# The first blocks of a fused layer: one tile of rows ahead of the rest, loads in another order

## The reference

```python
x = x + tanh(g_xattn[0]) * L0_xattn(layernorm(x), ctx, ctx)   # softmax over q^T k / 16, per tile
x = x + tanh(g_ffn[0]) * L0_ffn(layernorm(x), W_syn, b_syn, W_out, b_out, gamma, beta)
x = x + tanh(g_xattn[1]) * L1_xattn(ctx, ctx, layernorm(x), ssm_kernel, D, 8)
x = x + tanh(g_ffn[1]) * L1_ffn(layernorm(x), gate_w, w_gate_up, w_down, ws_gate_up, ws_down)

# in L0_ffn
scale = mean(abs(W));  q = clip(round(W / (scale + 1e-8)), -1, 1) * scale   # ternary weights
z = x @ q.T + b_syn                                                         # 256 -> 1024, then the top 102 of a row are kept
out = layernorm(x + out, gamma, beta)
```

## Time and profile before

| | us |
|---|---|
| median of three runs | 744.54 |
| the profiled execution | 744.91 |
| its span | 742.8 |
| TensorE busy | 615.8 (83%) |
| VectorE busy | 478.2 (64%) |
| GpSimd busy | 433.9 (58%) |
| ScalarE busy | 285.2 (38%) |

### The profile page before, as it was taken

The page is one execution under the profiler, slowest core; times in us unless marked ns, Lnnn a source line. Parts: engine busy times, 40 slices in busy tenths (PEclk is TensorE's granted clock), DMA queues, the critical chain, the costliest instruction groups (busy, mean ns, idle before and its releaser), DMA issues.

```text
span 742.8 us, 12155 instructions
## 1 busy us (share of the span) xinstructions
PE 615.8 (83%) x3072; PEld 474.9 (64%) x3072; DVE 478.2 (64%) x1604; ACT 285.2 (38%) x641; POOL 433.9 (58%) x482
## 2 busy tenths in 40 slices
PE   3699994863998966999999649999999999999920
PEld 2355552532887744777777538888888888888620
DVE  3898997998687768688886433444455454455415
ACT  2146777873353432254444303233223223232200
POOL 2487997230244330677777651676767777777660
PEclk9999997897999987999999678999999999999965
DMA  6358655697387936476673379999999999997958
GB/s 216 106 188 263 225 190 199 213 318 278 116 328 258 386 100 235 156 243 214 218 235 137 106 245 302 264 247 238 251 257 248 242 265 252 263 248 161 233 85 310
DMA packets 89035, 167.84 MB, mean 226 GB/s; under 512 B 11280, under 2 KB 53712, under 8 KB 88976
## 3 DMA queue, kind: packets, MB, share of 16 engines
q1 hardware_dynamic: 67504, 138.44, 56.1%
q0 software_dynamic: 20608, 27.82, 18.9%
q10 hardware_dynamic: 864, 0.93, 0.3%
HBM read 93.33 MB, written 73.81 MB: 225 GB/s over the span
## 4 chain that ended last, share of the span: by engine, by line
PE 60%; DVE 17%; issue 9%; DMA 7%; POOL 3%; ACT 2%; DVEq 1%; SPq 0%; POOLq 0%; ACTq 0%
PE psum L1103 11%; PE psum L1021 6%; PE psum L1116 6%; PE psum L1107 5%; PE psum L942 5%; PE psum L1121 4%; PE psum L1087 3%; PE psum L863 3%; DVE hh L1679 3%; PE psum L1032 3%; DMA acc<-hh,toki 2%; POOL acc L806 2%; PE psum L978 2%; PE psum L933 2%; PE psum L835 1%
## 5 line engine op out<-in xcount | busy, mean ns | idle before, releaser
L806 POOL DMA_INDIRECT acc<-hh,toki x128 | 187.9, 1468 | 84.3 <-DVE hh L1994 47.9
L1994 DVE TENSOR_SCALAR hh<-psum,wtok 96x256 f32<-96x256 f32 (+3 forms) x128 | 55.9, 477 | 133.0 <-issue 118.2
L766 POOL DMA_INDIRECT xs_rows<-Z,slot x96 | 96.4, 1004 | 43.6 <-issue 26.0
L1103 PE MATMUL psum<-qT,Z 128*128 128x192 f32 (+3 forms) x480 | 99.8, 351 | 0.0
L1103 PEld LDWEIGHTS psum<-qT,Z 128*128 128x128 f32 x480 | 82.3, 193 | 2.9
L684 POOL TENSOR_TENSOR rstd<-mv,neghalf 128x1 f32<-128x1 f32 (+1 forms) x48 | 35.5, 739 | 80.0 <-DVE mv L1439 64.6
L1372 ACT ACTIVATE qT<-psum 128x384 f32<-128x384 f32 (+3 forms) x64 | 33.5, 523 | 97.0 <-PE psum L1087 96.1
L863 PE MATMUL psum<-wt,hTs 128*128 128x512 f32 x128 | 59.5, 607 | 0.6 <-ACT hTs L1201 0.6
L942 PE MATMUL psum<-wt,hh 128*128 128x256 f32 x256 | 57.9, 379 | 0.0
L1116 PE MATMUL psum<-Z,hh 128*96 128x256 f32 (+3 forms) x240 | 56.7, 379 | 0.0
L1107 PE MATMUL psum<-qT,Z 128*112 128x192 f32 (+3 forms) x240 | 53.5, 345 | 0.0
(11 more groups left out here) (350 smaller groups left out, 1257.8 us busy)
## 6 DMA issues: line engine op xcount, KB each, us to landing
Z<-in_wexp SPq DMA_DIRECT2D x62, 496.0 KB, 4.4
xs_rows<-fill SPq DMA_DIRECT2D x64, 272.0 KB, 3.2
kv_rows<-Z SPq DMA_DIRECT2D x12, 688.0 KB, 3.7
kvb<-kv_rows SPq DMA_DIRECT2D x8, 688.0 KB, 6.3
Z<-co_rows SPq DMA_DIRECT2D x8, 688.0 KB
Z<-kv_rows SPq DMA_DIRECT2D x8, 688.0 KB, 6.5
Z<-xs_rows SPq DMA_DIRECT2D x24, 204.0 KB, 3.9
Z<-xs_rows SPq DMA_DIRECT2D x16, 272.0 KB, 3.9
```

The source lines that it names most:

```text
L766: pool.indirect_dma_start(out=xs_rows[:, :], out_offset=bass.IndirectOffsetOnAxis(ap=slot[:, t, k:k + 1], axis=0), in_=H[:, t, :], in_offs ...
L806: pool.indirect_dma_start(out=acc[a][:, :], out_offset=bass.IndirectOffsetOnAxis(ap=toki[0:p, g, j:j + 1], axis=0), in_=y_sb[0:p, s, j, :] ...
L1103: m = pe.matmul(pA[par][:, g * CAP:g * CAP + 2 * p], w[:, s, k, g * P:(g + 1) * P], xT[:, par, k, 0:2 * p], start=(k == 0), stop=(k == 1))
L1994: m = dve.tensor_scalar(y_sb[0:p, s, j, :], pY[par][0:p, j * D:(j + 1) * D], wtok[0:p, g, j:j + 1], None, ALU.mult)
```

## The change

X's first load is split: tile 0 alone (semaphore `x_first`), then the context of tile 0, then tiles 1 to 3. W^T follows the context of tile 1 as before, but tiles 4 to 7 of X move behind the context of tile 2, and tiles 8 to 15 a block later. Gamma, beta and bout move from ScalarE's queue to SP's, behind W^T; bsyn moves there too, between the loads of the heads 0 and 1 of `ctxH`. D stays with ScalarE. The moments take any range of tiles, written out instead of looped; tile 0's are taken alone, and GpSimd powers it alone. VectorE's blocks -1 to 2 are written out in a new function, `first_tiles`; the moments of tiles 4 to 7 go to the end of block 2, the lower cut stays at the end of block 1 and the upper cut moves into block 2. TensorE's sum over ones moves ahead of `scores(2)`. The gate weights signal `ws_in` instead of a semaphore of their own.

```diff
-            load_x(0)
+            sp.dma_start(X[:, 0, :], x[0]).then_inc(x_first, 16)
             load_ctx(0, 0)
+            sp.dma_start(X[:, 1:4, :], x[1:4].rearrange("b p d -> p b d")).then_inc(x_in[0], 16)
             load_ctx(1, 1)
             sp.dma_start(wraw[0], wsynT.rearrange("(k p) n -> p k n", p=P)).then_inc(wraw_in, 16)
-            load_x(1)
+            for dst, src, n in ((gam_b, gamma, D), (bet_b, beta, D), (bout_b, bout, D)):
+                sp.dma_start(dst[:, :], bc(src, n)).then_inc(small_in, 16)
             for b in range(2, NT):
                 sp.wait_ge(sc_done, b - 1)
                 sp.wait_ge(v_scaled, b - 1)
                 load_ctx(b, b % 2)
                 if b == 2:
+                    load_x(1)
                     load_ctxH(0)
+                    sp.dma_start(bsyn_b[:, :], bc(bsyn, N)).then_inc(small_in, 16)
                     load_ctxH(1)
-                if b in (2, 3):
-                    load_x(b)
+                if b in (3, 4):
+                    load_x(b - 1)
...
-            pow_input(0)
+            pow_input(0, 1, 1)
+            pow_input(1, 4, 2)
...
-                if there(b + 1):
-                    scores(b + 1, 1 - par)
                 if type(b) is int and b == 1:
                     pe.wait_ge(wabs_ready, 1)
                     pe.matmul(psum[:, 7, 0:1], onesf[:, :], wabs[:, 0:1], start=True, stop=True).then_inc(ones_done, 1)
+                if there(b + 1):
+                    scores(b + 1, 1 - par)
...
-            for dst, src, n in ((gam_b, gamma, D), (bet_b, beta, D), (bout_b, bout, D), (D_b, ssm_D, NH),
-                                (bsyn_b, bsyn, N)):
-                act.dma_start(dst[:, :], bc(src, n)).then_inc(small_in, 16)
+            act.dma_start(D_b[:, :], bc(ssm_D, NH)).then_inc(small_in, 16)
...
-            input_moments(0)
+            input_moments(0, 1, x_first)
...
+            def first_tiles(b, par):
+                if b == -1:
+                    input_moments(1, 4, x_in[0])
+                    reduced = highest(0, 0)
+                    exponent_shift(0, 0, reduced)
+                    query(1, 1)
+                elif b == 0:
+                    query(2, 0)
+                    divided = divisors(0, 0)
+                    scale_v(0, 0, divided)
+                elif b == 1:
+                    reduced = highest(1, 1)
+                    exponent_shift(1, 1, reduced)
+                    query(3, 1)
+                    add1(0, 0)
+                    summed = stats1(0)
+                    aggregated = aggregate1(0, summed)
+                    divided = divisors(1, 1)
+                    variance1(0, aggregated)
+                    scale_v(1, 1, divided)
+                    weight_scale(0, psum[:, 7, 0:1])
+                    below_cut(0)
+                else:
+                    reduced = highest(2, 0)
+                    exponent_shift(2, 0, reduced)
+                    add1(1, 1)
+                    summed = stats1(1)
+                    above_cut(0)
+                    aggregated = aggregate1(1, summed)
+                    divided = divisors(2, 0)
+                    variance1(1, aggregated)
+                    scale_v(2, 0, divided)
+                    gated()
+                    norm_h(0, 0)
+                    input_moments(4, 8, x_in[1])
+                    query(4, 0)
```

More of the change, by code:

```diff
@@ L260, in build @@
         x_in = [sem(f"x_in{c}") for c in range(4)]
+        x_first = sem("x_first")
         gates_on, small_in = sem("gates_on"), sem("small_in")
@@ L322, in build @@
         l_step = sem("l_step")
-        gate_in = sem("gate_in")
         ws_in = sem("ws_in")
@@ L487, in _ @@
             load_early(1)
-            sp.dma_start(gate_sb[:, :, :], gateT).then_inc(gate_in, 16)
+            sp.dma_start(gate_sb[:, :, :], gateT).then_inc(ws_in, 16)
             sp.dma_start(wsd_sb[:, 0:2, :], wsd[0:2 * P, :].rearrange("(c p) d -> p c d", p=P)).then_inc(ws_in, 16)
@@ L656, in _, with pow_input @@
                       allow_small_or_imprecise_dtypes=True).then_inc(consts, 1)
-            def pow_input(c):
-                pool.wait_ge(var_ready, c + 1)
-                pool.tensor_tensor(rstd[:, 4 * c:4 * c + 4], mv[:, 4 * c:4 * c + 4, 1], neghalf[:, 0:4], ALU.pow).then_inc(rstd_ready, 1)
+            def pow_input(first, last, done):
+                pool.wait_ge(var_ready, done)
+                pool.tensor_tensor(rstd[:, first:last], mv[:, first:last, 1], neghalf[:, first:last], ALU.pow).then_inc(rstd_ready, 1)
             pool.memset(tri[:, :], 1.0)
@@ L708, in first_blocks @@
                 if b in (2, 4, 5):
-                    pow_input({2: 1, 4: 2, 5: 3}[b])
+                    c = {2: 1, 4: 2, 5: 3}[b]
+                    pow_input(4 * c, 4 * c + 4, c + 2)
                 if there(b - 1):
@@ L1039, in _ @@
             pe.wait_ge(qT_ready, NT)
-            pe.wait_ge(gate_in, 16)
             pe.wait_ge(c_done, 4)
-            pe.wait_ge(ws_in, 48)
+            pe.wait_ge(ws_in, 64)
             for v_ in range(1, NPAIR + 1):
@@ L1424, in tiles @@
                 v["at"], v["k"] = start + (hi_ - lo_) * per, 0
-            def run(first, last, body):
-                with dve.Fori(first, last) as t:
-                    body(t).then_inc(v_step, 1)
-                v["k"] += last - first
-                dve.wait_ge(v_step, v["at"] + v["k"])
             def moments(src, t, signal):
@@ L1439, in moments, with input_moments @@
                 dve.tensor_tensor(mv[:, t, :], mvt[:, 0, :], eps2[:, :], ALU.add).then_inc(signal, 1)
-            def input_moments(c):
-                dve.wait_ge(x_in[c], 16)
+            def input_moments(first, last, arrived):
+                dve.wait_ge(arrived, 16)
                 alone(dve, "dve")
-                run(4 * c, 4 * c + 4, lambda t: dve.bn_stats(stats[:, t, :], X[:, t, :]))
+                for t in range(first, last):
+                    m = dve.bn_stats(stats[:, t, :], X[:, t, :])
+                link(m)
                 alone(dve, "dve")
-                for t in range(4 * c, 4 * c + 4):
+                for t in range(first, last):
                     m = dve.bn_aggr(mvt[:, t, :], stats[:, t, :])
                 link(m)
-                dve.tensor_tensor(mv[:, 4 * c:4 * c + 4, :], mvt[:, 4 * c:4 * c + 4, :], eps2[:, None, :].to_broadcast([P, 4, 2]),
+                dve.tensor_tensor(mv[:, first:last, :], mvt[:, first:last, :], eps2[:, None, :].to_broadcast([P, last - first, 2]),
                                   ALU.add).then_inc(var_ready, 1)
@@ L1482, in out_weight_sums @@
                 dve.tensor_reduce(wabs[:, 1:2], wraw[1], AX.XY, ALU.add, apply_absolute_value=True).then_inc(wabs_ready, 1)
-            def ternary(w):
-                below_cut(w)
-                above_cut(w)
             def below_cut(w):
@@ L1497, in query @@
             def query(b, par):
-                if type(b) is int and b % 4 == 0 and b < NT - 3:
-                    dve.wait_ge(rstd_ready, b // 4 + 1)
+                if type(b) is int and b == 1:
+                    dve.wait_ge(rstd_ready, 2)
+                elif type(b) is int and b % 4 == 0 and b < NT - 3:
+                    dve.wait_ge(rstd_ready, b // 4 + 2 if b else 1)
                 if later(b):
@@ L1558, in keep_z @@
                                          bsyn_b[:, :].rearrange("p (a n) -> p a n", a=2), ALU.mult, ALU.add).then_inc(z_ready, 1)
+            def first_tiles(b, par):
[34 more added lines that the diff above has]
+                    query(4, 0)
             def first_blocks(b, par):
                 early = b if type(b) is int else -9
-                if early == 2:
-                    input_moments(1)
-                    gated()
+                if early in (-1, 0, 1, 2):
+                    first_tiles(early, par)
+                    return
                 if early in (4, 5):
-                    input_moments(early - 2)
+                    input_moments(4 * early - 8, 4 * early - 4, x_in[early - 2])
                 if early == NT + 1:
@@ L1581, in first_blocks @@
                 if early == 5:
-                    dve.wait_ge(rstd_ready, 4)
+                    dve.wait_ge(rstd_ready, 5)
                 if there(b):
@@ L1593, in first_blocks @@
                     keep_z(b - 4, par)
-                if early == 1:
-                    weight_scale(0, psum[:, 7, 0:1])
-                    ternary(0)
                 if early == 3:
```

## The result

The changed kernel takes 740.25 us (median of 4 runs, 739.47 to 740.38) against 744.39 for the kernel before on the same chip (743.57 to 745.19): ratio 0.9938, interval 0.9925 to 0.9951. That is 4.14 us by the medians and 4.6 by the ratio (0.0062 x 744.39). The profiled execution took 740.13 us with a span of 738.3, against 742.8 before: 4.5 us less. The prediction was 741.0 (739.3 to 743.4).

What follows compares the result with a forecast made beforehand. It took a serial start chain (X's load, moments, power, query, scores) to bound what precedes block 5, with later blocks at fixed pace. Of 4.5 us gained, 3.5 arrive past GpSimd: 744.54 - 3.5 = 741.0 us, range 739.3 to 743.4.

Steps and rivals of the forecast that it cites:

- rival of a larger gain: At block 5: GpSimd through sooner, VectorE's own 4.5 us arrive, or X lands at 3.0; 739.3 us, chance 0.10.
- First tile alone: Kernel start: X's first tile lands at 4.1, query 0 at 5.9, highest score of tile 0 at 8.65 against 12.45.
- Tiles 1 to 3: X's second load: lands at 6.8 if rates hold; its moments end at 8.6, just beside the scores.
- The rival built on it: At the start: tiles 1 to 3 land at 8.9, everything 2.1 us later; 743.1 us, chance 0.07.
- Weights sooner: Weights' load: lands at 11.4 instead of 14.57; ScalarE's sum ends at 13.5, before TensorE asks at 14.2.
- Bias rows through SP at nothing: SP's queue: 384 KB behind the weights and 512 KB between head loads cost nothing; covers 1, 5 and 8 us.
- the choke: SP's queue: bias rows slow in themselves, 384 KB until 18, second batch at about 31; 749 us, chance 0.04.
- VectorE's order: Blocks 1 and 2: lower cut to add1 of tile 2 takes 11.15 against 11.53; that add1 at 28.3, 4.1 sooner.
- the first two steps: Tile 0 alone, then query 1 behind it: add1 of tile 0 at 14.25 instead of 17.53, 3.3 us gained.
- Straight code at tiles 8 to 11: VectorE's moments of these tiles, written out instead of looped: up to 0.4 us more gained.
- GpSimd takes over: Block 5: VectorE must wait for GpSimd's power until 44.7, resuming at 44.85; of 4.5 us, 3.5 arrive.
- The clock: TensorE: higher level near 29; as a rival, a further block runs low, 4.2 us more, 745.2 us, chance 0.03.

Runs made afterwards that it cites:

- rows_act: Changed kernel with the four broadcast bias rows back in ScalarE's queue, tiles 4 to 15 of X still late; 742.57 us, ratio 0.9962.
- tile_only: Kernel before with only X's first load split and tile 0's moments and power taken alone; 745.02 us, ratio 1.0002.
- old_order: Changed kernel with VectorE's blocks -1 to 2 and the ones matmul in the old order, loads and split kept; 741.84 us, ratio 0.9956.
- products_early: Changed kernel with GpSimd computing the products of heads 0 and 1 after block 1 instead of behind blocks 2 and 3; 741.06 us, ratio 0.9948.
- query_later: Changed kernel with the query of tile 4 moved from the end of block 2 into block 3; 739.41 us, ratio 0.9927.
- x_whole: Changed kernel with X's tiles 0 to 3 in one load again, tile 0's moments still alone; 741.67 us, ratio 0.9960.
- old_loads: Changed kernel with bias rows back in ScalarE's queue and tiles 4 to 15 in their old places, split and order kept; 743.67 us, ratio 0.9983.
- tiles_sooner: Changed kernel with only tiles 4 to 15 of X back in their old load places, rows staying in SP's queue; 739.79 us, ratio 0.9926.
- weights_act: Changed kernel with the 1024 KB of weights asked for from ScalarE's queue at its start instead of SP's; 742.17 us, ratio 0.9967.

## Why the prediction was right, and where not

The time (740.25) lies between the forecast (741.0) and the rival of a larger gain (739.3). That it came so near is in part luck: VectorE reached add1 of tile 2 1.37 us sooner than reckoned (26.93 against 28.3), 0.4 us expected behind it did not come, and the 1.0 us put down to GpSimd were lost to something else. Step by step:

- *First tile alone*: right, a little low. X's first tile lands near 3.7 (asked for at 0.78, 2.9 us), forecast 4.1; query 0 at 5.52, forecast 5.9; highest 0 at 8.16, forecast 8.65.
- *Tiles 1 to 3*: landed by 6.03, forecast 6.8. The dip from 6 to 7 us came from ScalarE's rows and not from the start itself: with them back in that queue there is such a dip (112 GB/s from 4 to 5 in rows_act), in the changed kernel there is none before the rows' own time from 9 us on. The rival built on it fell, but tile_only shows that it was the right rival for a kernel in which the rows stay: there highest 0 is even later than before.
- *Weights sooner*: right. 11.28, forecast 11.4. The cover was thinner than said: the sum over the weights ends 0.03 us behind mix 0, where 0.7 was forecast.
- *Bias rows through SP at nothing*: right in the sum, and the choke's own premise was half true. The rows are slow in themselves (149 and 125 GB/s from full engines, where 315 was reckoned), but the last of the three lands at 12.6 and not at 18, and the 512 KB row at 18.5 and not at 31. VectorE waits for none of them: the gate products run at 21.91 with no wait ahead. TensorE does stand 2.38 us, until 19.93, for the context of tile 3, which was asked for behind the 512 KB row, but VectorE reads those scores only at 26.33, with no wait. The strict order that the step took for the queue didn't hold: gamma landed at 10.9, ahead of the weights (11.28) that stand before it.
- *VectorE's order*: the stretch from the lower cut to add1 of tile 2 is 11.10, forecast 11.15. The step put all the gain of the order there, and left what the new order does ahead of the lower cut to the first two steps. old_order shows 1.86 of its 2.30 us to lie there. Add1 of tile 2 came 5.51 us sooner instead of 4.1, since what stands ahead of the lower cut came 1.12 us sooner than estimated (15.83, forecast 16.95) and add1 of tile 1 found mix 1 done, where a wait was reckoned.
- *Straight code at tiles 8 to 11*: put at up to 0.4 us, gained nothing. The four statistics are shorter (1.39 against 1.76), but from their start to block 5's reciprocal it is 11.64 us against 11.58 before.
- *GpSimd takes over*: the step that failed. Its size was right, 1.07 us given back between add1 of tile 2 and block 5 where 1.0 was forecast, but not its mechanism. VectorE does not wait for GpSimd there: the power ends at 43.70, ScalarE's exponentials at 43.80, and the wait of 0.38 is for ScalarE, as before. GpSimd's own row of work was sized well (18.75 us from its power at 24.95, forecast 18.35), but it began 1.4 us sooner, because the last moment step of tiles 4 to 7 falls at 24.71 and not at 26.1; so far the first half of the larger-gain rival came true. What is late is VectorE itself, whose work in block 3 runs beside GpSimd's products and takes longer: from add1 of tile 2 to the moments of tiles 8 to 11 it is 5.34 us here and 4.33 both in old_order (29.23 to 33.56) and before (32.44 to 36.77), 1.01 of the 1.07. The two scalings are 0.77 of it (1.24 against 0.47); the exponent's shift ahead of them (0.67 against 0.16) and the query (0.83 against 0.65) are longer too, and later small steps give a little back. products_early, which takes the products out of block 3, brings the stretch back to 4.33. The forecast wait is real but lies one step further on, as query_later shows.
- *The clock*: as forecast. The expand matmuls at 25.14 take 3.75 us for four (the lower level, 1.2 GHz), the scores at 28.68 1.21 (the higher, 2.4); the change of level was put near 29.

One step was never made: to ask whether the parts add. They don't. At block 5 the split alone gives -0.56 and the loads alone -0.71, and together, in old_order, 3.20; the third part, the order, adds 1.24 on top of them. The order without the other two was not run. The rows fit two waits in parallel: the split alone leaves VectorE and TensorE waiting for tiles 1 to 3 and the context, the loads alone leave it waiting for X.

Behind block 5 the times do not follow block 5 closely: x_whole is 2.63 us later than the changed kernel at block 5 and 1.6 at the end (by the ratios), rows_act 3.21 and 0.0024 x 744 = 1.8, old_loads 3.30 and 0.0045 x 744 = 3.3. Each interval is some 2 us wide, and executions of one kernel lie up to 4.1 us apart (tiles_sooner, 737.48 to 741.55), so whether the middle stages give back part of a loss, or the runs merely scatter, was not found out.

## What to carry to other kernels

At a serial start, list every transfer in flight with its queue before splitting a load: the split paid only once the broadcast rows had left the second queue and stood behind the weights. Ask of each pair of edits whether both remove a wait in front of the same instruction; if so, neither shows alone. When an engine is made early, look which instructions it will then run beside: the rows of VectorE's scalings were short or long by what GpSimd did at that moment.

## What was not expected of the hardware

- A small first load starts the stream earlier: in the microsecond from 2 to 3 us tile_only moves 131 GB/s and the kernel before, whose first load is four times as large, 33.
- 1 KB rows broadcast to 128 partitions leave the engines 0.46 to 0.54 busy when they come from ScalarE's queue beside SP's loads (rows_act), and while they are in flight in SP's queue (changed kernel, 9 to 11 us) full engines move no more than 125 to 149 GB/s. The packets differ: 0.04 us each in ScalarE's queue, with idle time between them, but some 0.15 us each from 9 to 11 us of the changed kernel (214 packets, the weights' last 25 among them, in 98.8% of 16 engines' 2 us).
- A 1024 KB load in ScalarE's queue took 94.2% of the engines from 4 to 6 us and left SP's 5.3% (weights_act).
- A tenth of the weights comes late. Their 1024 KB are 256 packets of 4 KB; in the changed kernel 25 of these (the packets of more than 2 KB) start only between 9 and 10.8 us, and the load lands at 11.28. In tiles_sooner, where whole rows of X follow them instead of broadcast ones, it is 29 packets and 11.43, so the broadcast rows are not the cause. What holds them back was not found out.
- GpSimd's power takes 0.58 us for one column, 0.87 for three and 1.01 for four.
